# Attention's reciprocals: spread by a DMA of ScalarE's queue in place of a VectorE shuffle, and sent ahead of the next row of maxima

## The chip, the cores and the metric

The kernel runs on one core of a Trainium2 chip. The metric is the device time of one execution in microseconds (us), the median of three runs. A profile comes from one more execution, and its trace gives each instruction's start and duration on TensorE (PE, with its weight loads PEld), VectorE (DVE), ScalarE (ACT), GpSimd (POOL) and SyncE, whose work here is to issue DMAs (SP).

## The reference

A transformer layer of float32 on x of shape (2, 512, 512): attention with 32 heads of 16 columns behind a layer norm, then a mixture of 8 experts (two per token, 800 hidden columns) behind another.

```python
q, k, v = (proj(w_q), proj(w_k), proj(w_v))
scores = jnp.einsum('bhqd,bhkd->bhqk', q, k) / jnp.sqrt(jnp.float32(D_K))
attn = jax.nn.softmax(scores, axis=-1)
out = jnp.einsum('bhqk,bhkd->bhqd', attn, v)
...
x = x + _L0_attn_ref(_layernorm(x, axis=-1), L0_attn_w_q, L0_attn_w_k, L0_attn_w_v, L0_attn_w_o)
x = x + _L0_ffn_ref(_layernorm(x, axis=-1), L0_ffn_gate_w, L0_ffn_w1, L0_ffn_w2, L0_ffn_w3)
```

## The kernel before, in words

The first 97 us compute q, k and v, the last 280 us the experts. Between them lies the attention stage, in 16 head groups (`NG`) of four heads of one batch entry. Every engine has its own program, written out by hand, and engines wait for each other by semaphores that count. For one head group g:

- TensorE multiplies keys and queries once for the row maxima: 16 blocks of 128 x 512 (`key_max`, L762), into one of three banks of PSUM. VectorE reduces each block to 128 negated maxima (`maximum`, L1450). A transpose (`max_t`, L753), a copy by ScalarE (`maxima`, L1184, to max_rows) and two DMAs of SyncE (L487) lay them as one more row of the stacked queries.
- TensorE multiplies again, with keys in the rows and the maximum taken off by that row (`scores`, L774): 8 pairs of matmuls, into two pairs of banks in turn. ScalarE takes the exponential of each pair (L1234, 128 x 1024), 8 to a group. A pair of banks is free again for the scores two further when its exponential is done.
- TensorE multiplies the exponentials with the values (`pv`, L743): four P·V blocks, into ps_o. v_ones holds a column of ones beside each column of v, so the odd rows of ps_o carry the sums of the softmax.
- ScalarE copies ps_o to o_raw (L1219). SyncE brings the sums of four heads from o_raw to sum_rec, 128 x 16 (L501). VectorE takes the reciprocal (L1510). SyncE lays the reciprocals out as four rows of rec_row, 1 x 512 each, in partitions 1, 33, 65 and 97 (L495). VectorE's `stream_shuffle` (L1525) copies each of them to the 32 partitions around it, into rec_all.
- GpSimd multiplies o_raw by rec_all (L645, o_norm), SyncE brings the even partitions of o_norm into o_all, kept in q_hi's memory (L522), and GpSimd splits pairs of groups for the projection behind the stage (L659, L661).

All of this runs as a pipeline over steps s. In step s TensorE and ScalarE work on scores and exponentials of group s, VectorE on the maxima of group s + 2, and the reciprocals are those of group s - 2. TensorE's order is the list `steps` of pairs (a, b): a counts quarters of the maxima, b quarters of the scores, and in each pair TensorE issues two `key_max`, one P·V block, one `key_max`, two score matmuls, one `key_max` and two score matmuls. Up to pair 28 (`AHEAD`) both counts are equal. There a quarter without maxima is put in, and from then on the scores run one quarter ahead of the maxima. In steps 2 to 7 (groups 0 to 5) the reciprocal therefore falls one quarter before the third exponential of its step; in steps 8 to 13 (groups 6 to 11) it falls into the same quarter.

ScalarE's order in a step: exponentials 1 and 2, o_raw of the group before, (in the first half the copy of the maxima's row,) exponential 3, 4, (in the second half that copy,) exponentials 5 to 8.

SyncE's order in a step: the maxima's row of group s + 1, the reciprocals' row of group s - 2, the sums of group s - 1, up to 12 transfers of the next stacks of q and k (128 KB each), the transfer of o_norm of group s - 2, and in steps 14 and 15 a load of half of x1 from HBM (1 MB, L531), which VectorE's `residual` (L1491) waits for. SyncE waits in this order too: for the maxima's row before it looks at the reciprocals.

## Time and profile before

| | |
|---|---|
| median of three runs | 565.57 us (565.06 to 565.7) |
| the profiled execution | 566.67 us, span 564.9 us |
| TensorE busy | 539.6 us (96%) |
| VectorE busy | 393.6 us (70%) |
| ScalarE busy | 324.4 us (57%) |
| GpSimd busy | 126.0 us (22%) |
| attention stage | about 97 to 283 us |

The span is the time from the first to the last instruction in the trace; the execution's own time has 1.8 us more around it. Busy shares are averages over the whole program. Matmuls are pipelined and their ends are modelled, so TensorE's busy time holds short waits as well; the idle time of its weight loads (PEld) shows what it waited for. Start and duration of a DMA instruction are those of its issue by the engine's queue; when the data have landed is seen in the chain of waits, as "DMA".

### The profile page before, as it was taken

To read this page: it belongs to the slowest core of one execution; us is meant where nothing else is said; L and a number is where in the kernel's file an instruction comes from. 1 tells how busy PE (TensorE), PEld (TensorE's weight loads), DVE (VectorE), ACT (ScalarE), POOL (GpSimd) and SP (SyncE) were. 2 spreads that over 40 slices of the span, in tenths; PEclk is the share of its full clock that TensorE was granted. 3 is DMA by queue.
4 is the path that set the end of the run, shared out by engine and by line. 5 is a ranking of instruction groups with operands and counts; after the bars stand their busy time and mean duration, and the time that the engine had idled before them with its cause. 6 is when DMAs were issued, how large, how long until landed. Compare 5 with 4: busy or idle time off the path is not lost.

```text
span 564.9 us, 9754 instructions
## 1 busy us (share of the span) xinstructions
PE 539.6 (96%) x3504; PEld 391.7 (69%) x3504; DVE 393.6 (70%) x730; ACT 324.4 (57%) x480; POOL 126.0 (22%) x153
## 2 busy tenths in 40 slices
PE   7999999999999999999998999999999999999991
PEld 6887665333333333333667988999999999999981
DVE  6915656999998999971689887664828465666650
ACT  4322114778778777777246463747657565757540
POOL 3300111000230202452201203234341321331202
PEclk9999998999999999999999999999999999999997
DMA  8290367927456762002384499594664758586122
GB/s 317 112 112 1 56 90 80 114 42 92 71 87 80 88 82 89 20 14 87 109 303 130 175 337 351 147 329 77 248 189 140 268 148 282 99 291 170 43 32 36
DMA packets 31117, 78.19 MB, mean 138 GB/s; under 512 B 9693, under 2 KB 10973, under 8 KB 26587
## 3 DMA queue, kind: packets, MB, share of 16 engines
q1 hardware_dynamic: 25770, 68.84, 46.4%
q0 software_dynamic: 5296, 8.69, 8.4%
q8 instruction: 30, 0.49, 0.4%
q14 instruction: 21, 0.16, 0.1%
HBM read 53.11 MB, written 9.32 MB: 111 GB/s over the span
## 4 chain that ended last, share of the span: by engine, by line
PE 73%; DVE 12%; DMA 6%; issue 3%; POOL 2%; ACT 1%; SPq 1%; POOLq 0%; ACTq 0%; DVEq 0%
PE ps L731 15%; PE ps L733 14%; PE ps L732 14%; DVE neg_max L1450 7%; PE ps_o L743 7%; PE ps L762 6%; PE ps_m L762 3%; PE ps L774 3%; DMA rec_row<-sum_rec 2%; PE ps L799 2%; DMA x<-x 1%; DMA w_sb<-w 1%; DVE rec_all L1525 1%; POOL o_norm L645 1%; PE ps_o L731 1%
## 5 line engine op out<-in xcount | busy, mean ns | idle before, releaser
L1234 ACT ACTIVATE probs_t<-ps 128x1024 f32<-128x1024 f32 x128 | 124.1, 1022 | 36.1 <-PE ps L774 35.5
L1450 DVE TENSOR_REDUCE neg_max<-ps 128x1 f32<-128x512 f32 x170 | 111.7, 684 | 12.3 <-PE ps L762 10.2
L731 PE MATMUL ps<-xgT_hi,w_hi 128*128 128x256 f32 (+7 forms) x384 | 110.9, 289 | 0.9 <-DVE xgT_lo L1712 0.8
L733 PE MATMUL ps<-xgT_hi,w_lo 128*128 128x256 f32 (+7 forms) x384 | 109.7, 286 | 0.0
L732 PE MATMUL ps<-xgT_lo,w_hi 128*128 128x256 f32 (+7 forms) x384 | 109.7, 286 | 0.0
L762 PE MATMUL ps<-k_stack,q_stack 48*128 48x512 f32 x170 | 71.5, 459 | 3.6 <-issue 1.1
L731 PEld LDWEIGHTS ps<-xgT_hi,w_hi 128*128 128x128 f32 x384 | 72.7, 189 | 1.7 <-DVE xgT_lo L1712 1.3
L732 PEld LDWEIGHTS ps<-xgT_lo,w_hi 128*128 128x128 f32 x384 | 72.8, 189 | 0.1
L733 PEld LDWEIGHTS ps<-xgT_hi,w_lo 128*128 128x128 f32 x384 | 72.7, 189 | 0.0
L743 PE MATMUL ps_o<-probs_t,v_ones 128*32 128x512 f32 x512 | 68.2, 605 | 0.0
L1729 DVE TENSOR_TENSOR act<-gate,ps 128x256 f32<-128x256 f32 (+7 forms) x48 | 20.7, 431 | 67.2 <-PE ps L733 51.4
L762 PEld LDWEIGHTS ps<-k_stack,q_stack 48*128 48x128 f32 x170 | 28.8, 185 | 52.9 <-DVE neg_max L1450 41.8
L774 PE MATMUL ps<-q_stack,k_stack 49*128 49x512 f32 x256 | 63.3, 431 | 0.4 <-ACT probs_t L1234 0.4
L1450 DVE TENSOR_REDUCE neg_max<-ps_m 128x1 f32<-128x512 f32 x86 | 58.9, 684 | 4.5 <-PE ps_m L762 4.1
L1555 DVE TENSOR_TENSOR w_lo<-w_sb,w_hi 128x1024 fp32r<-128x1024 f32 x48 | 56.5, 1218 | 0.0
L1308 ACT ACTIVATE gate<-ps 128x256 f32<-128x256 f32 (+7 forms) x48 | 18.8, 392 | 61.2 <-PE ps L733 60.4
L1256 ACT ACTIVATE w_hi<-w_sb 128x1024 fp32r<-128x1024 f32 x48 | 48.6, 1056 | 3.7 <-DMA w_sb<-w 3.6
L645 POOL TENSOR_TENSOR o_norm<-o_raw,rec_all 128x512 f32<-128x512 f32 x15 | 19.2, 1283 | 101.8 <-DVE rec_all L1525 101.8
L762 PE MATMUL ps_m<-k_stack,q_stack 48*128 48x512 f32 x86 | 39.9, 464 | 1.1 <-DMA q_stack<-max_rows 0.4
L774 PEld LDWEIGHTS ps<-q_stack,k_stack 49*128 49x128 f32 x256 | 30.9, 187 | 12.0 <-ACT probs_t L1234 8.6
L691 POOL DMA_INDIRECT out<-xn,to_now x20 | 33.8, 1691 | 6.5 <-issue 6.5
L762 PEld LDWEIGHTS ps_m<-k_stack,q_stack 48*128 48x128 f32 x86 | 15.9, 185 | 27.1 <-DVE neg_max L1450 22.9
(323 smaller groups left out, 984.9 us busy)
## 6 DMA issues: line engine op xcount, KB each, us to landing
w_sb<-w SPq DMA_DIRECT2D x16, 1024.0 KB
w_sb<-w SPq DMA_DIRECT2D x8, 1536.0 KB
w_sb<-w SPq DMA_DIRECT2D x8, 1152.0 KB
q_stack<-q_hi SPq DMA_DIRECT2D x32, 128.0 KB, 5.3
k_stack<-k_hi SPq DMA_DIRECT2D x32, 128.0 KB, 5.0
q_stack<-q_lo SPq DMA_DIRECT2D x16, 128.0 KB, 4.5
k_stack<-k_lo SPq DMA_DIRECT2D x16, 128.0 KB, 6.1
q_hi<-o_norm SPq DMA_DIRECT2D x16, 128.0 KB, 3.9
```

The source lines that it names most:

```text
L645: pool.tensor_tensor(o_norm[:, g % 2, :], o_raw[:, g % 2, :], rec_all[:, :], ALU.mult).then_inc(s_on, 1)
L691: pool.indirect_dma_start(out=out[:, :], out_offset=bass.IndirectOffsetOnAxis(ap=to_now[0:rows, m:m + 1], axis=0), in_=y_sb[0:rows, m, :], ...
L731: pe.matmul(o, x_hi, w_hi, start=start, stop=False)
L732: pe.matmul(o, x_hi, w_lo, start=False, stop=False)
L733: return pe.matmul(o, x_lo, w_hi, start=False, stop=stop)
L743: last = pe.matmul(ps_o[32 * j:32 * j + 32, :], v_ones[:, (g // 8) * TPB + kc, (g % 8) * GH + j, :, :].rearrange("p d o -> p (d o)"), prob ...
L762: pe.matmul(max_bank(g, u2), q[:, qt * P:(qt + 1) * P], k, start=True, stop=True).then_inc(s_sn, 1)
L774: last = pe.matmul(ps4[:, 2 * (n % 2) + c, :], k[:, kc * P:(kc + 1) * P], q, start=True, stop=True)
L1234: a.activation(probs_t[:, kc % 2, 2 * half:2 * half + 2, :], ps4[:, 2 * (n % 2):2 * (n % 2) + 2, :], ACT.Exp, scale=D ** -0.5).then_inc(s_ ...
L1256: a.activation(w13_hi[:, at], w13_sb[:, at], ACT.Copy).then_inc(s_hi13, 1)
L1450: v.tensor_reduce(neg_max[:, g % 2, col:col + 1], max_bank(g, u2), AX.X, ALU.max, negate=True).then_inc(s_mx, 1)
L1555: v.tensor_tensor(w13_lo[:, at], w13_sb[:, at], w13_hi[:, at].bitcast(f32), ALU.subtract).then_inc(s_lo13, 1)
```

## The change

ScalarE's program gets a DMA in each of steps 2 to 15, behind the third exponential: it waits for the reciprocals' row of group s - 2 and for the o_norm before, and copies each of the four rows 16 times, to the even partitions of rec_all (64 rows of 2 KB). GpSimd waits for that transfer in place of the shuffle. For the groups 14 and 15 the shuffle stays. GpSimd fills rec_all with ones once before, so that the odd partitions hold something. And SyncE's step begins with the reciprocals' row, ahead of the maxima's row. The semaphore s_wide counts the new transfers.

```diff
+SPREAD = NG - 2
+SPREAD_AT = 2
...
             for s in range(-4, NG + 2):
+                g = s - 2
+                if 0 <= g < NG:
+                    sp.wait_ge(s_rc, g + 1)
+                    if g >= 1:
+                        sp.wait_ge(s_wide, 16 * min(g, SPREAD))
+                    if g > SPREAD:
+                        sp.wait_ge(s_sh, g - SPREAD)
+                    sp.dma_start(rec_row[1:P:2 * D, :], sum_rec[:, g % 2, :]).then_inc(s_rb, 16)
                 g = s + 1
                 if 0 <= g < NG:
                     sp.wait_ge(s_mr, g + 1)
...
-                g = s - 2
-                if 0 <= g < NG:
-                    sp.wait_ge(s_rc, g + 1)
-                    if g >= 1:
-                        sp.wait_ge(s_sh, g)
-                    sp.dma_start(rec_row[1:P:2 * D, :], sum_rec[:, g % 2, :]).then_inc(s_rb, 16)
...
             prepare(3)
+            pool.memset(rec_all[:, :], 1.0).then_inc(s_ones, 1)
 
             for g in range(NG - 1):
-                pool.wait_ge(s_sh, g + 1)
+                if g < SPREAD:
+                    pool.wait_ge(s_wide, 16 * (g + 1))
+                else:
+                    pool.wait_ge(s_sh, g - SPREAD + 1)
...
                         a.activation(probs_t[:, kc % 2, 2 * half:2 * half + 2, :], ps4[:, 2 * (n % 2):2 * (n % 2) + 2, :],
                                      ACT.Exp, scale=D ** -0.5).then_inc(s_ex, 1)
+                    if u == SPREAD_AT and 0 <= s - 2 < SPREAD:
+                        g = s - 2
+                        a.wait_ge(s_rb, 16 * (g + 1))
+                        if g == 0:
+                            a.wait_ge(s_ones, RING + 1)
+                        else:
+                            a.wait_ge(s_on, g)
+                        a.dma_start(rec_all[0:P:2, :],
+                                    rec_row[1:P:2 * D, :].unsqueeze(1).broadcast_to([GH, D, S])).then_inc(s_wide, 16)
...
-                    if u2 == 11 and g >= 0:
+                    if u2 == 11 and g >= SPREAD:
                         v.wait_ge(s_rb, 16 * (g + 1))
-                        if g >= 1:
-                            v.wait_ge(s_on, g)
+                        v.wait_ge(s_on, g)
                         v.stream_shuffle(rec_all[:, :], rec_row[:, :], [1] * 32).then_inc(s_sh, 1)
 
-            v.wait_ge(s_sh, NG)
+            v.wait_ge(s_sh, NG - SPREAD)
```

On SyncE, around the border of two steps in the second half, the order before was (the line numbers are those of each kernel; a size stands behind the names of target and source):

```order
L522 DMA q_hi<-o_norm 64x512
L487 DMA q_stack<-max_rows 1x8x128 x2
L495 DMA rec_row<-sum_rec 4x32x16
L501 DMA sum_rec<-o_raw 128x1x16
L522 DMA q_hi<-o_norm 64x512
L525 DMA q_lo<-wo 128x2048
```

In the changed kernel it is:

```order
L527 DMA q_hi<-o_norm 64x512
L492 DMA rec_row<-sum_rec 4x32x16
L498 DMA q_stack<-max_rows 1x8x128 x2
L506 DMA sum_rec<-o_raw 128x1x16
L527 DMA q_hi<-o_norm 64x512
L530 DMA q_lo<-wo 128x2048
```

The reciprocals' row has moved up past the two DMAs of the maxima's row, and stands directly behind the transfer that ends a step.

On ScalarE, in a step of the second half, the order before was:

```order
L1219 ACTIVATE o_raw<-ps_o 128x512
L1234 ACTIVATE probs_t<-ps 128x1024 x2
L1184 ACTIVATE max_rows<-ps 16x128
L1234 ACTIVATE probs_t<-ps 128x1024 x6
L1219 ACTIVATE o_raw<-ps_o 128x512
```

In the changed kernel it is:

```order
L1228 ACTIVATE o_raw<-ps_o 128x512
L1243 ACTIVATE probs_t<-ps 128x1024
L1252 DMA rec_all<-rec_row 64x1x512
L1243 ACTIVATE probs_t<-ps 128x1024
L1193 ACTIVATE max_rows<-ps 16x128
L1243 ACTIVATE probs_t<-ps 128x1024 x6
```

The DMA stands between the third and the fourth exponential, and everything of ScalarE behind it waits when it waits.

## Rows read from the trace of the kernel before

**Rows 1.** The page: busy time, the chain that ended last, DMA issues

```profile
PE 539.6 (96%) x3504; PEld 391.7 (69%) x3504; DVE 393.6 (70%) x730; ACT 324.4 (57%) x480; POOL 126.0 (22%) x153
...
PE 73%; DVE 12%; DMA 6%; issue 3%; POOL 2%; ACT 1%; SPq 1%; POOLq 0%; ACTq 0%; DVEq 0%
PE ps L731 15%; PE ps L733 14%; PE ps L732 14%; DVE neg_max L1450 7%; PE ps_o L743 7%; PE ps L762 6%; PE ps_m L762 3%; PE ps L774 3%; DMA rec_row<-sum_rec 2%; PE ps L799 2%; DMA x<-x 1%; DMA w_sb<-w 1%; DVE rec_all L1525 1%; POOL o_norm L645 1%; PE ps_o L731 1%
...
k_stack<-k_lo SPq DMA_DIRECT2D x16, 128.0 KB, 6.1
```

**Rows 2.** Stretches: length, busy of each engine, clock, DMA share, GB/s

```profile
130.83:133.53 2.70, 2.62 (x19) 0.95 (x17) 2.70 (x5) 2.27 (x3) 0.00 (x0) 1.00 0.06 9
133.53:136.57 3.04, 3.00 (x18) 1.11 (x17) 3.04 (x7) 2.28 (x4) 1.28 (x1) 1.00 0.71 125
214.08:217.10 3.02, 2.92 (x18) 1.11 (x17) 3.02 (x7) 2.27 (x4) 1.46 (x2) 1.00 0.04 5
```

**Rows 3.** Groups of VectorE's instructions, 122 to 240 us

```profile
L1525 DVE STREAM_SHUFFLE rec_all<-rec_row 128x512 f32<-128x512 f32 x11 | 8.2, 747 | 0.0
```

**Rows 4.** TensorE in order of time: start, duration, line, count

```profile
210.81 0.40 PE L774 MATMUL ps<-q_stack,k_stack 49*128 49x512 f32 x1
...
212.37 0.73 PE L774 MATMUL ps<-q_stack,k_stack 49*128 49x512 f32 x2
```

**Rows 5.** ScalarE in order of time, first and second half

```profile
130.30 1.94 ACT L1234 ACTIVATE probs_t<-ps 128x1024 f32<-128x1024 f32 x2 [0.23 <-PE ps L774]
...
207.73 1.94 ACT L1234 ACTIVATE probs_t<-ps 128x1024 f32<-128x1024 f32 x2
210.34 0.27 ACT L1184 ACTIVATE max_rows<-ps 16x128 fp32r<-16x128 f32 x1 [0.67 <-PE ps L753]
...
213.21 1.94 ACT L1234 ACTIVATE probs_t<-ps 128x1024 f32<-128x1024 f32 x2 [0.44 <-PE ps L774]
```

**Rows 6.** VectorE in order of time

```profile
207.12 0.25 DVE L1510 RECIPROCAL sum_rec<-sum_rec 128x16 f32<-128x16 f32 x1
...
250.93 0.23 DVE L1510 RECIPROCAL sum_rec<-sum_rec 128x16 f32<-128x16 f32 x1
```

**Rows 7.** SyncE's DMA issues in order of time

```profile
130.09 1.45 SPq L487 DMA_DIRECT2D q_stack<-max_rows  x2
...
206.21 0.60 SPq L522 DMA_DIRECT2D q_hi<-o_norm  x1
210.63 1.44 SPq L487 DMA_DIRECT2D q_stack<-max_rows  x2
212.18 0.59 SPq L495 DMA_DIRECT2D rec_row<-sum_rec  x1
```

**Rows 8.** TensorE's weight loads in order of time, with idle and releaser

```profile
213.26 0.18 PEld L762 LDWEIGHTS ps<-k_stack,q_stack 48*128 48x128 f32 x1 [0.25 <-DMA q_stack<-max_rows]
```

**Rows 9.** The chain that ended last: start, duration, what

```profile
189.87 1.83 DMA rec_row<-sum_rec
...
256.23 1.29 POOL o_norm L645
...
258.10 7.14 DMA x<-x
...
266.81 1.29 POOL o_norm L645
...
269.35 4.89 DMA rec_row<-sum_rec
```

**Rows 10.** DMA, 249 to 253 us: packets and share; size and us to landing

```profile
DMA packets 80, 0.13 MB, mean 33 GB/s; under 512 B 16, under 2 KB 16, under 8 KB 80
...
q1 hardware_dynamic: 80, 0.13, 8.7%
...
q_hi<-o_norm SPq DMA_DIRECT2D x1, 128.0 KB, 2.6
```

**Rows 11.** ScalarE in order of time, 262.7 us

```profile
262.80 1.02 ACT L1234 ACTIVATE probs_t<-ps 128x1024 f32<-128x1024 f32 x1
```

More of the change, by code:

```diff
@@ L260, in moe_layer @@
         s_sh = sem("s_sh")
+        s_wide = sem("s_wide")
         s_on = sem("s_on")
```

## The prediction

> **What bounds the kernel now.** I read the page first [rows 1]: TensorE is busy for 96% of the span, VectorE for 70%, and the chain that ended last is 73% TensorE and 12% VectorE, with the row maxima (L1450) as VectorE's largest line. So TensorE is the bound, but VectorE stands in the chain. The change lies in the attention stage, so the next view was the table of stretches, cut at the starts of successive P·V blocks (L743), of which a head group has four [rows 2]. An ordinary stretch takes 2.70 us, the one with the shuffle 3.03, and VectorE is busy in all of it. The reader is to see that TensorE sets 2.70 us and that the 0.747 us shuffle [rows 3] adds only 0.33 us to a head group, since VectorE catches up in the other three stretches.
>
> Third, the order of time in one head group of the second half of the stage [rows 4 to 8]. ScalarE, SyncE and TensorE hang closely together there: ScalarE copies the maxima's row at 210.34, SyncE sends it at 210.63, and TensorE's first key block of the next group waits for it at 213.26, with 0.25 us of idle weight load. That wait has no slack. It is the most important thing in the profile for this change.
>
> Last, the chain from 255 us on [rows 9]: after the maxima end, the stage's end is set not by TensorE but by o_norm, the load of x1 and the reciprocals' rows, one after another.
>
> **The sum, part by part.** Times are of the profiled execution (span 564.9, own time 566.67); the differences are applied to the median of 565.57.
>
> *Shuffles taken away.* 14 of 16 go. 11 of them lie in 122 to 240 us [rows 3], where maxima run beside them: 11 x (3.03 - 2.70) = 3.6 us. The twelfth meets the last maxima and the other two none, with TensorE at work: nothing. Bounds: 3.6, and 0 if the 3.03 were TensorE's own need; but VectorE's 3.04 of 3.04 us speaks for the shuffle.
>
> *The reciprocals' row sent first.* SyncE ends the last transfer of its step (L522) at 206.81 and the reciprocal ends at 207.12 + 0.25 = 207.37 [rows 6, 7]. The old kernel then waits for the maxima's row and sends the reciprocals at 212.18. The new one sends them at 207.40, and a lone row lands 1.83 us later [rows 9], at 209.23. The maxima's row finds SyncE free again at 208.0, long before 210.63. The edit costs nothing by itself, since SyncE was idle.
>
> *The issue on ScalarE, first half (six groups).* The reciprocal comes a whole stretch before ScalarE's third exponential (L1234), so the wait is met when ScalarE reaches it. The exponential before the issue runs for 0.92 us (1.94 - 1.02, rows 5), and an issue of 0.59 fits behind it. I take 0. Below it nothing is to be had, as ScalarE loses no work; the most is 0.31 a group, worked out under the rivals.
>
> *The issue on ScalarE, second half (six groups).* Here ScalarE's steps run one stretch ahead of the maxima, so the third exponential falls into the stretch of the reciprocal itself. It starts at 207.73 and the fourth at 208.65 [rows 5]. ScalarE now waits behind the third until 209.23, and issues. No DMA is issued by ScalarE in this trace; nearest are SyncE's, 0.57 to 0.60 us each, 0.72 for one of the maxima's pair [rows 7]. Bounds 0 and 0.72; I take 0.59, that of the row that is sent to rec_row. The fourth exponential starts at 209.26 + 0.59 + 0.10 = 209.95 in place of 208.65, and ends 1.02 later, at 210.97. Two things wait for it. The second pair of score matmuls needs its bank; a pair takes 0.73 [rows 4], so it ends at 210.97 + 0.06 + 0.73 = 211.76, where it ended at 210.81 + 0.40 = 211.21: 0.55 late. And the copy of the maxima's row, next on ScalarE, starts at 209.95 + 0.92 = 210.87 in place of 210.34, 0.53 late, and TensorE already waits for that row [rows 8]. Both delays are the same time on TensorE, not two: 0.55. ScalarE makes it good before the next group, as it idles 0.44 us before the pair at 213.21. 6 x 0.55 = 3.3 us; with an issue of 0 us it is 0, with 0.72 it is 4.1.
>
> *The transfer and o_norm.* GpSimd now waits for 128 KB. The nearest row, a lone transfer of 128 KB, lands after 2.6 us [rows 10]. Of its 80 packets 64 are of 2 KB; 8.7% of 16 engines in 4 us is 0.087 us for each of these. The new source lies in 4 partitions. If it is spread over 4 engines in place of 16, each carries 16 packets and not 4: 12 x 0.087 = 1.0 more, 3.6 us. The upper bound is the 6.1 us of k_stack<-k_lo, last of six in a queue [rows 1]. I take 3.6: the queue of ScalarE is empty, so it is near the lone row, and its source is narrow. In the steady groups it is hidden: issued at 209.26 it lands at 212.9, before the stretch of the shuffle at 214.08.
>
> The Trainium skill (DMA: Bandwidth & Descriptors, section on why a DMA increments its semaphore by 16 and not by 1) says that the number of engines is the largest up to 16 that divides the slowest dimension of both sides; here these are 4 and 64, so 4. By that rule the 3.6 us stand, without it 2.6; no row here shows the engines of one transfer.
>
> *The tail.* The reciprocals of 250.93 end at 251.16 [rows 6], are sent at 251.19 and land at 253.02; ScalarE issues at 253.05, and at 256.65 they are spread. The o_norm of that group, at 256.23 before [rows 9], starts at 256.69. The load of x1 behind it moves from 258.10 to 258.56, and the next row goes 0.67 later, at 259.23. Behind such a load a row takes 4.89 [rows 9]: landed at 264.12. ScalarE waits for exactly this row in its next step, behind the third exponential of 262.80 [rows 11]; it issues at 264.15 and the spread lands at 267.75, where o_norm had started at 266.81: +1.0 us. From there the chain is serial to the end of the stage. TensorE is held too, as the fourth exponential starts at 264.84 and not at 263.72, but this is the same microsecond. Bounds of the term: with a landing of 2.6 us o_norm is at 255.7, the row lands at 263.1 and the next spread at 265.8, -1.0; with 6.1 us twice, +6.
>
> Sum: -3.6 + 0 + 3.3 + 1.0 = +0.7 us: 566.3 (profiled, 567.4). About 0.2%, 1.13 us, is the least that can be told from no change here.
>
> **The rivals.**
> *ScalarE's issue costs it almost nothing*: the exponentials go on beside it. Then the fourth starts at 209.4, the score pair and the maxima's row are on time, and the 3.3 become 0: -3.6 + 1.0 = -2.6, 563.0. For it: nothing in the trace shows what a compute engine pays. Against: SyncE pays near 0.6 for every size.
> *Sixteen engines*: the tail gives 1.0 back, -3.6 + 3.3 - 1.0 = -1.3, 564.3. Against it is only the narrow source.
> *The two queues get in each other's way, slower.* In the first half ScalarE's issue, at 130.30, falls into SyncE's two of the maxima's row, 130.09 to 131.54 [rows 5, 7]. If one can issue at a time, ScalarE's runs from 130.83 to 131.42, and the fourth exponential starts at 131.53, not 131.22: 0.31 us on TensorE, whose score pair waits for it, in the five groups where the rows meet: 1.5 us. It decides as soon as ScalarE's issue ends later than its third exponential. 566.3 + 1.5 = 567.8. For it: the issues stand close; against: no row has two queues issuing at once.
> The Trainium skill (Perfetto Trace Analysis, DMA Instruction — HWDGE) says that the block that makes descriptors is shared and locked for one engine at a time. That is this rival; by the rule the sum is 567.8, without it 566.3.
> *The shuffle's 0.33 does not come back*, because TensorE's own need fills it: 3.6 more, 569.9. VectorE's full stretch speaks against it.
> That the row isn't sent ahead at all, because SyncE still waits for o_norm of the step before, I exclude: that transfer ended at 206.81, and o_norm comes no later now.
>
> **How the numbers follow.** Forecast 0.38, its own range 565.3 to 567.4; cheap issue 0.22; sixteen engines 0.12; queues 0.18; no gain from the shuffle 0.06; anything else 0.04. Faster (under 564.44): the cheap issue, half of the sixteen engines, half of the rest and a tenth of the forecast, 0.32. Slower (over 566.70): queues, no gain, half of the rest and a quarter of the forecast, 0.36. Same: 0.32. The range runs from the cheap issue to the queues, 562.8 to 567.9; past it lie no gain from the shuffle, long landings and a part of the cheap issue, together 0.2.
>
> **What would show it.** Right: no stretch of 3.03 us; a DMA issue of ScalarE of about 0.6 us near 209, 0.6 to 1.3 us of idle ScalarE before the fourth exponential, and TensorE waiting 0.5 us for ScalarE or the maxima's row in each of six groups; o_norm 1 us later near 267 against the P·V blocks. Wrong: exponentials unmoved beside the issue (cheap issue), an issue of ScalarE or SyncE of over 1 us near 130 (queues), o_norm earlier near 267 (sixteen engines), or stretches still at 3.03. The term of which I am least sure is ScalarE's 0.59 us.

## The result, and the profile after

The changed kernel takes 588.27 us (median; 583.96 to 592.58), the kernel before 565.57: a ratio of 1.0396, 95% interval 1.0367 to 1.0425. It is slower by 22.7 us, where I had forecast + 0.7 and a range that ended at 567.9. The profiled execution is the fastest of the five: 583.96 us, span 582.2, mean granted clock 0.973. The slower ones have lower clocks (592.58 us at 0.951), so the loss has a part that varies with the clock.

The page, as in [rows 1]: busy time, the chain that ended last, its lines.

```profile
PE 543.9 (93%) x3504; PEld 393.0 (68%) x3504; DVE 387.0 (66%) x702; ACT 323.8 (56%) x480; POOL 126.6 (22%) x154
...
PE 67%; DMA 11%; DVE 7%; SPq 5%; issue 3%; POOL 2%; ACT 2%; ACTq 1%; POOLq 0%; DVEq 0%
PE ps L740 15%; PE ps L742 15%; PE ps L741 15%; DMA rec_row<-sum_rec 7%; PE ps_o L752 5%; DVE neg_max L1468 4%; PE ps L771 4%; SPq L481 3%; PE ps_m L771 2%; DMA q_stack<-max_rows 2%; PE ps L808 2%; DMA rec_all<-rec_row 1%; PE ps L783 1%; SPq L498 1%; POOL o_norm L654 1%
```

The busy times hardly differ. The chain does: the reciprocals' row has risen from 2% to 7%, SyncE's issues are on it with 5%, and VectorE has gone from 12% to 7%. The stretches between P·V blocks, with the columns of [rows 2]:

```profile
121.02:123.73 2.71, 2.63 (x18) 1.02 (x17) 2.49 (x5) 1.95 (x3) 1.27 (x1) 1.00 0.61 131
129.19:133.43 4.24, 2.41 (x19) 0.76 (x17) 2.81 (x5) 2.24 (x3) 0.00 (x0) 1.00 0.41 76
...
176.79:181.94 5.15, 3.03 (x20) 1.06 (x18) 2.67 (x4) 2.45 (x4) 0.00 (x0) 1.00 0.32 34
181.94:185.44 3.50, 3.50 (x19) 1.56 (x17) 2.76 (x5) 2.20 (x4) 1.28 (x1) 0.60 0.24 61
...
204.77:210.99 6.22, 3.48 (x19) 1.19 (x18) 2.69 (x5) 2.33 (x5) 0.00 (x0) 0.92 0.44 48
210.99:214.79 3.80, 3.71 (x19) 1.26 (x17) 2.46 (x4) 1.66 (x2) 1.27 (x1) 0.69 0.34 85
232.93:235.99 3.06, 3.04 (x19) 1.06 (x18) 2.66 (x5) 1.91 (x4) 0.00 (x0) 1.00 0.16 25
```

The first row is the place of a shuffle: 2.71 us where it was 3.03, as forecast. But the stretch with ScalarE's DMA is 4.24, 5.15 or 6.22 us, where 2.7 was forecast for the first half and 2.7 plus 0.55 for the second. Behind the two worst of them the next stretch is long too, with TensorE busy nearly throughout at a granted clock of 0.60 or 0.69. Only from 230 us on (last row) is it the small cost that I had expected.

Around the worst of them, SyncE's issues, ScalarE and TensorE in order of time, as in [rows 4, 5, 7]:

```profile
201.69 0.59 SPq L481 DMA_DIRECT2D k_stack<-k_lo  x1
202.33 0.60 SPq L527 DMA_DIRECT2D q_hi<-o_norm  x1
203.56 0.57 SPq L492 DMA_DIRECT2D rec_row<-sum_rec  x1
210.00 1.46 SPq L498 DMA_DIRECT2D q_stack<-max_rows  x2
```

```profile
203.89 1.03 ACT L1243 ACTIVATE probs_t<-ps 128x1024 f32<-128x1024 f32 x1
208.21 0.55 ACTq L1252 DMA_DIRECT2D rec_all<-rec_row  x1
208.81 1.02 ACT L1243 ACTIVATE probs_t<-ps 128x1024 f32<-128x1024 f32 x1 [3.89 <-DMA rec_row<-sum_rec]
```

```profile
209.88 0.74 PE L783 MATMUL ps<-q_stack,k_stack 49*128 49x512 f32 x2 [2.74 <-ACT probs_t L1243]
```

Here the row is sent as soon as it is made, as the change says, but ScalarE can issue only at 208.21: the row was on its way for 4.6 us and not 1.83. Its neighbours on SyncE show what has changed: the last of six stack transfers of 128 KB is issued 1.9 us before it, and o_norm's 1.2 us. The kernel before sent it 6 us behind the transfer that ends the step [rows 7]. The chain gives its durations over the stage, as in [rows 9]:

```profile
126.80 4.28 DMA rec_row<-sum_rec
149.94 5.29 DMA rec_row<-sum_rec
...
203.56 4.63 DMA rec_row<-sum_rec
...
242.90 1.81 DMA rec_row<-sum_rec
```

At 242.90 there are no more stacks to send, and it is 1.81 us again.

### The profile page after: what moved, and what is told of

It reads as the page before. It is cut to its first block, busy times and chain, and to the rows that moved or that the text cites. A ratio compares the mean times of both kernels' runs of the same rounds, so it can differ in the third digit from the quotient of the medians.

```text
span 582.2 us, 9742 instructions
## 1 busy us (share of the span) xinstructions
PE 543.9 (93%) x3504; PEld 393.0 (68%) x3504; DVE 387.0 (66%) x702; ACT 323.8 (56%) x480; POOL 126.6 (22%) x154
## 3 DMA queue, kind: packets, MB, share of 16 engines
q10 hardware_dynamic: 952, 1.84, 1.6%
## 4 chain that ended last, share of the span: by engine, by line
PE 67%; DMA 11%; DVE 7%; SPq 5%; issue 3%; POOL 2%; ACT 2%; ACTq 1%; POOLq 0%; DVEq 0%
PE ps L740 15%; PE ps L742 15%; PE ps L741 15%; DMA rec_row<-sum_rec 7%; PE ps_o L752 5%; DVE neg_max L1468 4%; PE ps L771 4%; SPq L481 3%; PE ps_m L771 2%; DMA q_stack<-max_rows 2%; PE ps L808 2%; DMA rec_all<-rec_row 1%; PE ps L783 1%; SPq L498 1%; POOL o_norm L654 1%
## 5 line engine op out<-in xcount | busy, mean ns | idle before, releaser
L783 PE MATMUL ps<-q_stack,k_stack 49*128 49x512 f32 x256 | 65.3, 457 | 12.1 <-ACT probs_t L1243 12.1
L771 PE MATMUL ps<-k_stack,q_stack 48*128 48x512 f32 x170 | 69.6, 464 | 5.0 <-DMA q_stack<-max_rows 1.7
L752 PE MATMUL ps_o<-probs_t,v_ones 128*32 128x512 f32 x512 | 71.7, 633 | 0.0
```

What stands on the lines that cost most here:

```text
L752: last = pe.matmul(ps_o[32 * j:32 * j + 32, :], v_ones[:, (g // 8) * TPB + kc, (g % 8) * GH + j, :, :].rearrange("p d o -> p (d o)"), prob ...
L771: pe.matmul(max_bank(g, u2), q[:, qt * P:(qt + 1) * P], k, start=True, stop=True).then_inc(s_sn, 1)
L783: last = pe.matmul(ps4[:, 2 * (n % 2) + c, :], k[:, kc * P:(kc + 1) * P], q, start=True, stop=True)
```

## The experiments

Times are medians of runs beside runs of the kernel before. In four kernels (1, 6, 10, 15) other values reach the experts, whose share of the work then changes, so only the attention stage compares there. "The stage" is the time from the start of the first P·V block to the start of the last in the profiled run, by the table of stretches. It is one execution of each kernel, and the changed kernel's five executions lie 8.6 us apart as a whole, so a difference of stages is rough where TensorE stalls. Landings of the row and of the narrow transfer (ScalarE's, out of 4 partitions) are those of the last semaphore event that the trace records for them.

| kernel | stage us | its clock | ratio to before (95%) |
|---|---|---|---|
| before | 172.8 | 1.00 | |
| after | 188.3 | 0.95 | 1.0396 (1.0367 to 1.0425) |
| 3 row first | 172.4 | 1.00 | 0.999 (0.9969 to 1.001) |
| 6 no shuffle | 169.2 | 1.00 | |
| 9 row by ScalarE's queue | 173.1 | 1.00 | 1.0012 (0.9985 to 1.0038) |
| 5 wait alone | 181.2 | 0.96 | 1.0153 (1.0126 to 1.018) |
| 1 small stacks | 172.4 | 1.00 | |
| 10 small spread | 182.4 | 0.95 | |
| 15 wide source | 181.3 | 0.96 | |
| 13 first half alone | 185.5 | 0.94 | 1.0172 (1.014 to 1.0205) |
| 11, 12, 4: spread at 3, 4, 5 | 191.2, 196.0, 195.2 | 0.90 | 1.0314, 1.045, 1.0581 |
| 7 SyncE spreads | 184.9 | 0.95 | 1.0238 (1.0202 to 1.0273) |
| 8 SyncE spreads, other order | 187.8 | 0.94 | 1.043 (1.0385 to 1.0475) |
| 14 stacks behind the row | 199.1 | 0.89 | 1.0439 (1.04 to 1.0478) |
| 2 row by GpSimd | 217.2 | 0.86 | 1.0867 (1.0835 to 1.09) |
| 16 four rows, 6 groups | 171.5 | 1.00 | 1.001 (0.9992 to 1.0027) |
| 17 four rows, 5 groups | 170.8 | 1.00 | 0.9948 (0.9928 to 0.9967) |
| 18 four rows, 12 groups | 171.1 | 1.00 | 0.9952 (0.9932 to 0.9971) |

### Is the row late because of the stacks?

**1, small stacks.**

```diff
+                w = T // B if pair < RING else 64
...
-                            sp.dma_start(to[at][dst, :, :].bitcast(f32),
+                            sp.dma_start(to[at][dst, :, 0:w].bitcast(f32),
```

> The changed kernel, but from pair 4 of the stacked queries and keys on only 64 of the 512 columns are copied (16 KB in place of 128 KB for each of the transfers behind the sums; the scores of groups 8 to 15 are then computed from partly old stacks). Theory A (behind the stacks: the reciprocals' row is sent directly behind six 128 KB transfers of SyncE's queue and lands 3.6 to 5.3 us after its issue, ScalarE waits for it in order, TensorE for ScalarE, and the clock falls after the stalls): the row lands 1.8 to 2.3 us after its issue in every group, the P.V stretch with ScalarE's DMA is at most 3.1 us as in groups 11 to 13 of the changed kernel, the granted clock is 1.00 throughout the stage; 565.6 - 3.6 + 6 x 0.25 + 1.0 = 564.5, range 562.5 to 567. Theory B (two issuing queues in each other's way, whatever the sizes): the stretches of 3.6 to 6.2 us stay, 580 or more. Theory C (ScalarE's issue or its own transfer is the cost): the time stays over 575.

The row lands after 1.80 to 2.14 us in groups 0 to 12. From step 2 to step 7 there is no long stretch at all, the clock is 1.00, and steps 8 to 13 show the price of ScalarE's issue itself, 2.94 to 3.02 us where a stretch of this place takes 2.75:

```profile
205.22:208.20 2.98, 2.98 (x18) 1.05 (x18) 2.58 (x5) 1.90 (x4) 1.88 (x2) 1.00 0.14 29
```

Theory A is right, C is out as the main cause. But C is not nothing. Two more stretches are long, 3.39 us at 185.29 and 3.23 at 208.20, because TensorE waits there for the maxima's row, as shown under 10 and 15. The stage takes 172.4 us against 172.8 before, so even with a prompt row the change gains next to nothing. The time of the whole (608.58) says nothing.

**3, row first.** The new order of SyncE in the kernel before, shuffle kept.

> The kernel before with SyncE's new order alone: the reciprocals' row ahead of the maxima's row, the spreading still by VectorE's shuffle at its old place. Theory A: the row lands late here too, 3.6 to 5 us after its issue where stacks are in the queue, but nobody waits for it in order until the shuffle, over 6 us later; TensorE and the clock are as before and the time is 565.6, range 564.5 to 566.5. A rival, by which the row's place disturbs the maxima's row (which TensorE waits for without slack): the maxima's row lands later, up to 0.5 us in each of six groups, 568.5.

563.56 against 564.13 us: the same. The rows of groups 1 to 9 land after 3.85 to 4.54 us, those of groups 10 to 12, behind no stacks, after 1.81 to 1.83. When the late ones are sent, three to five large transfers have not yet landed. So the order alone makes the row late and costs nothing while nobody waits for it.

**5, wait alone.**

```diff
+                    if u == 2 and 0 <= s - 2 < NG - 2:
+                        a.wait_ge(s_rb, 16 * (s - 1))
```

> The kernel before with the reciprocals' row sent first, as in experiment 3, and one wait more: behind the third exponential ScalarE waits for that row, and does nothing with it. No DMA on ScalarE, no spreading transfer, VectorE's shuffles all there. Theory A (the late row, waited for in ScalarE's order, is what costs): the first P.V stretches of the groups are 3.6 to 6 us where stacks are on their way, as in the changed kernel, the granted clock falls behind the worst of them, and the time is 563.6 + 15 to 25 = 578 to 590. Theory C (the issue and the 128 KB transfer cost, the wait alone is nothing): 565.

573.83 us, + 9.1, where 578 to 590 was expected; the stage is 8.8 us longer than with the row first. Step 8:

```profile
184.39:188.94 4.55, 3.02 (x19) 1.06 (x18) 2.70 (x5) 1.91 (x4) 1.60 (x2) 1.00 0.38 35
188.94:192.23 3.29, 3.29 (x19) 1.58 (x17) 2.75 (x6) 2.20 (x4) 0.29 (x1) 0.65 0.11 29
192.23:196.39 4.16, 4.16 (x18) 1.65 (x17) 3.05 (x6) 1.94 (x4) 1.27 (x1) 0.50 1.00 133
196.39:200.40 4.01, 4.01 (x18) 1.65 (x17) 2.65 (x6) 2.38 (x4) 0.00 (x0) 0.53 0.73 75
```

TensorE waits for an exponential and the stretch is 1.8 us longer than in 3. Then three stretches run at a granted clock of 0.65, 0.50 and 0.53; 0.50 is 1.2 GHz, the lower of its two levels, and this stretch takes 4.16 us there in place of 3.02 in 3. The three stalls of this run come to 5.0 us and the slow stretches behind them to 3.9. But all three lie in the second half: in the first, where ScalarE comes to the wait later, there is none, and the changed kernel has four (4.24, 3.61, 4.21 and 5.15 us). Half of its loss was thus not explained.

**2 and 9, the row by another queue.** In 2 GpSimd sends the row of groups 0 to 13 in the changed kernel; in 9 ScalarE sends that of groups 0 to 5 in experiment 3, from an empty queue.

```diff
+                    if u == 0 and 0 <= s - 2 < NG // 2 - 2:
+                        g = s - 2
+                        a.wait_ge(s_rc, g + 1)
...
+                        a.dma_start(rec_row[1:P:2 * D, :], sum_rec[:, g % 2, :]).then_inc(s_rb, 16)
```

> The changed kernel, with the reciprocals' row of groups 0 to 13 sent by GpSimd's queue, as soon as the reciprocal is there; SyncE sends the last two. ScalarE's DMA stays behind the third exponential, the six stack transfers stay in SyncE's queue. Theory A1 (the row is late because it stands behind the stacks in the same queue): it lands 1.9 to 2.8 us after its issue with the stacks still on their way, ScalarE's wait behind the third exponential shrinks from up to 3.9 us to at most 1 us in the second half and to nothing in the first, and the time is 565 to 570. Theory A2 (the row is late because the 16 DMA engines are busy with the stacks, from whatever queue it comes): it lands 3.6 to 5 us after its issue as before, and the time stays at 580 or more. Theory B (two queues): three queues now issue, 588 or more.

> Experiment 3 (row first, shuffle kept), but in steps 2 to 7 the reciprocals' row is issued by ScalarE, ahead of its first exponential, at the moment at which SyncE issued it there (125.30 us for group 1); ScalarE's queue is empty. Theory A1 (late because of its own queue, behind the stacks in order): the rows of groups 1 to 5 land after 1.8 to 1.9 us. Theory A2 (late because the DMA engines serve the stacks of all queues): they land after 3.5 to 4.5 us as in experiment 3. The time is that of experiment 3 within 1.5 us either way, as the shuffle comes 6 us later.

In 9 (565.44, ratio 1.0012, interval 0.9985 to 1.0038) the rows of groups 1 to 5 land 4.70, 4.16, 4.13, 4.00 and 3.81 us after their issue, in 3 it is 4.36, 4.14, 4.12, 3.93 and 3.85. The queue makes no difference: I had taken the row to stand behind the stacks in SyncE's own queue, and that is refuted. The packets of the row sent at 125.97 show where its time goes. The first line is the DMA of 9 from 125.97 to 128.90 us, the second its ScalarE queue (q10) from 128.90 to 129.70; columns are packets, MB, share of 16 engines:

```profile
q1 hardware_dynamic: 196, 0.33, 106.2%
...
q10 hardware_dynamic: 132, 0.01, 30.6%
```

For 3.0 us after its issue the empty queue moves nothing, while SyncE's transfers fill the engines. All its packets fall between 128.97 and 129.67, and the row has landed at 130.67. A lone row of 3 (sent at 227.83) has its first packet after 1.2 us and lands 0.3 us behind its last. So most of the delay lies ahead of the row's own data, and about 0.7 us behind them. The Trainium skill (DMA: Bandwidth & Descriptors, Queues, rings and completion order) says that the semaphore write of a DMA lands only after every earlier write of the same DMA engine, across its queues. The trace agrees in that the row is late from an empty queue too (4.70 us), but this rule bears on the last 0.7 us alone; why the packets start late was not looked into further. Experiment 2 (613.05 us, where 565 to 570 was expected) shows the same for GpSimd's queue: 5.4 us for the row sent at 174.62 beside stacks issued from 172.45 to 176.28, 2.2 us for the one sent at 188.61 without. It also sends late, behind GpSimd's other work, so its time tells nothing more.

### What does the spreading transfer do?

**10 and 15, fewer bytes; as many from a wide source.** The first spreads 64 of 512 columns. The second moves 128 KB to the same 64 partitions, but out of 64 and not out of 4.

```diff
-                                    rec_row[1:P:2 * D, :].unsqueeze(1).broadcast_to([GH, D, S])).then_inc(s_wide, 16)
+                                    rec_row[1:P:2, :]).then_inc(s_wide, 16)
```

> The changed kernel, but ScalarE's transfer spreads only 64 of the 512 columns (16 KB in place of 128; o_norm is divided in an eighth of its columns only). Its issue, ScalarE's wait for the row and the order are as in the changed kernel. The stage (first P.V block to the end of the last) took 172.4 us with the row first and shuffles, 188.3 in the changed kernel, 181.2 with the wait alone. Theory D (the rest of the cost comes from the transfer's length: it makes o_norm late, SyncE waits for o_norm before it sends the next row, and so the next row is late as well): the stage takes about 181.2 - 3.3 + 6 x 0.25 = 179.4 us, rows are sent every 11 us and land after 4.1 us. The rival (the length does not matter, the issue on ScalarE does): 186 to 189.

> The changed kernel, but ScalarE's transfer of 128 KB reads 64 partitions of rec_row, one for each row of rec_all, in place of 4 partitions 16 times (the size and the target are the same, most of what it spreads is no reciprocal, so o_norm is not divided rightly). What is open is whether the transfer's 4.2 to 6.2 us, and SyncE's stack issues of 2.0 us beside it, come from its bytes or from its narrow source. By the narrow source: it lands after 2.6 to 3.5 us, SyncE's issues are 0.6 us, the first half is nearly clean, and the stage takes 182 to 184 us as with an eighth of the columns. By its bytes: 186 to 189 us and long issues as in the changed kernel.

The stage takes 182.4 and 181.3 us, near the 181.2 of the wait alone and 6 to 7 less than in the changed kernel. In the changed kernel the transfer takes 4.2 us alone and up to 6.2 beside stacks; here it is 1.83 to 2.12 in 10, and in 15

```profile
rec_all<-rec_row ACTq DMA_DIRECT2D x7, 128.0 KB, 2.0
```

(the last number is the median from issue to landing). The trace has 5 semaphore events for each narrow transfer, the first of them within 1 us of the start of its issue, and 16 for each wide one. That the other four are those of four engines is the rule that the prediction drew on, and the landings bear it out. What I had not foreseen is what it does to other DMAs. First to SyncE's issues, in the changed kernel and then in 15, behind ScalarE's issue at 131.10 and 132.40:

```profile
130.62 0.64 SPq L481 DMA_DIRECT2D q_stack<-q_hi  x1
131.30 0.59 SPq L481 DMA_DIRECT2D k_stack<-k_hi  x1
131.93 2.05 SPq L481 DMA_DIRECT2D q_stack<-q_lo  x1
134.03 2.04 SPq L481 DMA_DIRECT2D k_stack<-k_hi  x1
136.11 0.59 SPq L481 DMA_DIRECT2D q_stack<-q_hi  x1
```

```profile
133.77 0.59 SPq L481 DMA_DIRECT2D k_stack<-k_hi  x1
134.41 0.59 SPq L481 DMA_DIRECT2D q_stack<-q_lo  x1
135.04 0.60 SPq L481 DMA_DIRECT2D k_stack<-k_hi  x1
135.69 0.60 SPq L481 DMA_DIRECT2D q_stack<-q_hi  x1
```

While the narrow transfer is on its way two of SyncE's issues take 2.05 us and not 0.6. In the whole stage 9 of 48 issues that fall into such a flight take over 1.3 us, and none of 21 and 25 in 10 and 15. But the narrow transfer is not the only cause: one of 1.92 us stands at 124.13, where the first transfer had landed at 122.30, and experiment 6, which spreads nothing, has the same one:

```profile
123.77 1.86 SPq L478 DMA_DIRECT2D k_stack<-k_lo  x1
```

Second, the landing itself makes o_norm late, and SyncE sends o_norm before the next row. The transfer of 131.10 lands at 137.27, and the next row, whose reciprocal ends at 137.60, goes at 139.26:

```profile
137.33 1.28 POOL L654 TENSOR_TENSOR o_norm<-o_raw,rec_all 128x512 f32<-128x512 f32 x1 [13.68 <-DMA rec_all<-rec_row]
...
138.64 0.52 SPq L527 DMA_DIRECT2D q_hi<-o_norm  x1
139.26 0.58 SPq L492 DMA_DIRECT2D rec_row<-sum_rec  x1
```

In the changed kernel the rows of groups 2 and 4 wait like this for o_norm and those of groups 1, 3 and 5 for SyncE's issues, 0.5 to 1.7 us behind their reciprocals; in 3, 10 and 15 each of them goes at once. That brings the row to ScalarE's wait in the first half too.

Third, the maxima's row, which TensorE awaits without slack. In the second half it is sent while the narrow transfer is in flight and lands 2.0 to 2.6 us after its second issue, where it is 1.8 in 10 and 15. TensorE waits 2.7 us for it in the stage, against 0.4 in the kernel before and 0.5 in 10 and in 15.

The issue at 131.30 overlaps ScalarE's at 131.10 and neither is longer, and so it is at 142.89, 155.25 and 265.91. The rival of the prediction said that the two queues lock each other out in issuing, as the Trainium skill has it (Perfetto Trace Analysis, DMA Instruction — HWDGE); no such lengthening is seen here.

**13, first half alone.** `SPREAD = NG // 2 - 2`.

> The changed kernel with ScalarE's spreading for groups 0 to 5 alone; from group 6 on the shuffle, as before. By the theory as it stands (stacks in flight make the row land after 4 us; ScalarE is not held in the first half by that alone; the spreading transfer, 4.2 us alone and 5 to 6 beside the next stacks, makes o_norm and then the next row late): the first half loses what it loses in the changed kernel, 1.5 + 0.9 + 1.5 us and some clock, less 5 x 0.33 for the shuffles; the second half is that of the kernel before. 564.6 + 4 to 5 - 1.6 = 567.5, range 566 to 570. If the loss were in the second half alone: 563.

574.31 us, ratio 1.0172; expected 567.5. The mechanism is there (rows sent late, landing after 3.6 to 4.2 us, stretches of 4.39, 4.20, 3.54 and 5.30), the size is not: I had left most of the clock out once more. Behind the last stall stand four stretches of 4.16 to 4.90 us at a granted clock of 0.50.

### Where in the order could it stand?

**7 and 8, SyncE spreads.** In both ScalarE's DMA is gone and groups 12 to 15 keep the shuffle. In 7 the order is row, maxima's row, spread, sums, stacks, o_norm; in 8 maxima's row, row, o_norm of the group before, sums, spread, stacks.

```diff
+                if 0 <= s - 2 < SPREAD:
+                    g = s - 2
+                    sp.wait_ge(s_rb, 16 * (g + 1))
...
+                    sp.dma_start(rec_all[0:P:2, :],
+                                rec_row[1:P:2 * D, :].unsqueeze(1).broadcast_to([GH, D, S])).then_inc(s_wide, 16)
```

> The changed kernel with the spreading transfer of groups 0 to 11 issued by SyncE, behind the maxima's row and ahead of the sums; ScalarE issues and waits for nothing; groups 12 to 15 keep the shuffle. The reciprocals' row is still sent first and still lands 4 us after its issue. Theory A: only SyncE waits for it, where it idles anyway, so TensorE sees nothing: 564.1 - 3.6 + 0 to 1 = 561.0, range 559.5 to 564. The rival (the transfer, 4.2 us alone and 6 beside stacks, makes o_norm so late that SyncE reaches the next maxima's row late): 0.5 to 2 us in each of 12 groups, 570 or more.

> The kernel before with the spreading by a SyncE transfer for groups 0 to 11, ordered so that nothing waits where it hurts: the maxima's row, the reciprocals' row (alone on its way as in the kernel before, 1.83 us), the o_norm transfer of the group before, the sums, then the spreading transfer, then the stacks. No shuffle beside the maxima, no DMA on ScalarE. Theory A: every wait of SyncE is met, stretches of 2.70 to 2.76 throughout, the granted clock 1.00: 564.1 - 3.6 = 560.5, range 559.5 to 562.5. The rival, that a 128 KB transfer from four partitions beside the stacks is late whoever issues it and holds SyncE or o_raw up: 566 or more.

577.87 us (ratio 1.0238) and 588.24 us (1.043), both far off the 561.0 and 560.5 expected. The rivals won, each with its own wait. In 7 the sums now stand behind a wait and reach VectorE late; in 8, where most rows land after 1.84 us, o_norm is late for o_raw of the next group but one, which shares its buffer:

```profile
DVE sum_rec L1528 <- DMA sum_rec<-o_raw: 6.3, 6, 2.3
```

```profile
ACT o_raw L1242 <- POOL o_norm L668: 15.9, 9, 3.1
PE ps_o L766 <- ACT o_raw L1242: 7.6, 6, 2.1
```

(Waits: who, for whom; us in all, times, longest.) The spread takes 4.3 us in 7 and 4.2 to 5.4 in 8; the row lands after up to 5.6 us in 7.

**4, 11, 12, the place on ScalarE.** `SPREAD_AT` = 5, 3 and 4.

> The changed kernel with ScalarE's DMA behind the sixth exponential of its step in place of the third (one number). Theory A: the sixth exponential ends 3.9 us or more after the third, so the row, which lands 3.6 to 5.3 us after its issue, is there or nearly; ScalarE waits 0 to 0.5 us, no P.V stretch is over 3.2 us, the granted clock is 1.00; o_norm comes 3 us later in the tail. 565.6 - 3.6 + 0 to 1.5 for the issues + 2.5 for the tail = 565.0, range 562.5 to 567.5. Theory B or C (queues or the issue and transfer themselves): the cost doesn't depend on the place, 580 or more.

> The changed kernel with ScalarE's DMA behind the fourth exponential in place of the third. Theory A with two bounds: too early, ScalarE waits for the late row; too late, o_raw of the next group waits for o_norm. Here in the first half no wait, as the fourth exponential ends 0.9 us later than the third; in the second half the wait is 1 us shorter. Between the changed kernel (third, 584 to 588) and nothing lost: 570 to 580, I say 576.

> The changed kernel with ScalarE's DMA behind the fifth exponential. Theory A with two bounds: in the second half the fifth ends at about 211.8 on the clock of the kernel before, when the row (sent 207.4, 4.1 us) has landed, so no wait; issued at 211.8 the transfer lands at 216.5 to 217.5, o_norm ends at 218.3, and o_raw, which waits for it, is due at 218.2: just met. In the first half o_norm ends 1 us or more too late for o_raw. 568 to 580, I say 573; behind the sixth it was 598 (in time with the kernel before at 564.1). If ScalarE's place did not matter, 585.

597.96, 583.72 (1.0263 to 1.0365) and 593.65 us. My numbers were 565, 576 and 573: wrong by 33, 8 and 21 us, in the direction that a second bound exists. ScalarE's wait for the row shrinks (3.4 us in 4, 14.7 in the changed kernel), but the o_norm deadline is missed:

```profile
ACT o_raw L1228 <- POOL o_norm L654: 10.8, 8, 3.3
```

With a narrow transfer none of the four places tried lies between the two bounds. For 12 I had taken 4.7 to 5.7 us; beside stacks it was 4.5 to 6.9.

**14, stacks behind the row.** As 13, with the stacks ahead of the maxima's row in steps 2 to 7.

```diff
+                if 2 <= s < NG // 2:
+                    if s % 2 == 0:
+                        ready((s + 6) // 2)
+                    stack((s + 6) // 2, [s % 2], "qk")
                 g = s + 1
```

> As experiment 13, with one change of order on SyncE in steps 2 to 7: the six stack transfers stand directly behind the reciprocals' row, ahead of the maxima's row, in a gap in which SyncE idled. So no stack is in flight when the next row is sent, and the spreading transfer overlaps only their end. The maxima's row goes 1.3 us later, but has 5.7 us to spare in this half. Theory: rows 1 to 5 land after 1.8 to 2.3 us, the spread after 4.2 to 5, no stall in the first half, no shuffle in it: 564.6 - 5 x 0.33 = 563.0, range 562 to 564.3. Rival (the spreading transfer or ScalarE's issue costs by itself in this half): 566 or more.

589.29 us, where 563.0 was expected. The row does land after 1.81 to 1.89 us, but the maxima's row has taken its place behind the stacks, and TensorE waits for that one up to 5.1 us:

```profile
PE ps L775 <- DMA q_stack<-max_rows: 13.5, 4, 5.1
```

My 5.7 us of slack were wrong. Taking a small transfer out of the stacks' way by putting another into it is no gain.

### The ceiling, and versions that are faster

**6, no shuffle.**

```diff
-                    if u2 == 11 and g >= 0:
+                    if u2 == 11 and g >= NG - 2:
```

> The kernel before without the 14 shuffles of groups 0 to 13 and with nothing in their place: o_norm of these groups is multiplied by ones, so they are not divided by their sums; the reciprocals' rows are still sent. It gives the most that the change could bring. My sum said 11 x 0.33 = 3.6 us: 560.5 against 564.1. The rival, by which the 3.03 us stretches are TensorE's own need, says 564.1.

The stage takes 169.2 us, 3.6 less than in the kernel before and 3.3 less than in 3: all that the change could bring.

**16, 17 and 18, four rows.** SyncE writes the row of reciprocals four times, so that the spread reads 16 partitions. 16 does so for groups 0 to 5 behind the fourth exponential, 17 for groups 0 to 4, 18 for groups 0 to 11, behind the fifth from step 7 on.

```diff
+                    for c in range(4 if g < SPREAD else 1):
+                        sp.dma_start(rec_row[1 + 8 * c:P:2 * D, :], sum_rec[:, g % 2, :]).then_inc(s_rb, 16)
...
-                                    rec_row[1:P:2 * D, :].unsqueeze(1).broadcast_to([GH, D, S])).then_inc(s_wide, 16)
+                                    rec_row[1:P:8, :].unsqueeze(1).broadcast_to([4 * GH, D // 4, S])).then_inc(s_wide, 16)
```

> A version that takes the causes away in the half in which ScalarE has slack: ScalarE's spreading for groups 0 to 5 alone, behind the fourth exponential, from 16 partitions: SyncE writes the reciprocals' row four times (to partitions 1, 9, 17 and 25 of each head), in the 3 us in which it idles ahead of the maxima's row. From group 6 on the row goes once and the shuffle stands. If the narrow source is the cause of the long transfer and of SyncE's long issues: the last row is sent at +1.9 us and lands 4 us later, at the end of the fourth exponential, the spread takes 2.6 to 3.5 us, nothing is late, 564.3 - 5 x 0.33 = 562.7, range 561.5 to 564.5. If not, or if the four rows hold the maxima's row up: 568 or more, near the 574.3 of experiment 13.

> As experiment 16, for groups 0 to 4 alone. In 16 one stretch of 3.83 us stood in step 7, where the maxima's copy on ScalarE waited behind the DMA for the row (that step has the quarter in which the order of scores and maxima shifts); the rest of the half was at 2.70. Without group 5 that stretch is gone and one shuffle comes back: 171.5 - 1.07 + 0.3 = 170.8 us for the stage against 172.4, and 564.2 - 1.5 = 562.7, range 561.5 to 564.

> As experiment 16, for groups 0 to 11: behind the fourth exponential in steps 2 to 6 and behind the fifth from step 7 on, where the fourth copy of the row, sent 1.8 us after the first, has landed (209.0 against a first one sent at 204.65). All 11 shuffles beside maxima are gone, - 3.6. The issue pushes the sixth exponential back by 0.55, at 0.25 us on TensorE in each of six groups, + 1.5; stage 170.3, time 562.1, range 560.5 to 565. Rival: the four row issues leave SyncE no room ahead of the maxima's row, which TensorE waits for without slack: 0.5 or more in each of six groups, 566 or more.

16 takes 565.26 us, where 562.7 was expected: its stage takes 171.5, its first half runs at the ordinary length but for one stretch of 3.84 us in step 7, and the whole is the same as before within the measurement. 17 takes 561.85 us and 18 562.38: both are faster than the kernel before by half a per cent, with intervals that leave out 1, and not told apart. A stretch of 17 that had a shuffle, and its SyncE with four rows in the gap:

```profile
132.82:135.51 2.69, 2.62 (x17) 1.02 (x16) 2.47 (x5) 2.06 (x3) 0.84 (x1) 1.00 1.01 171
```

```profile
126.15 2.34 SPq L493 DMA_DIRECT2D rec_row<-sum_rec  x4
129.38 1.40 SPq L499 DMA_DIRECT2D q_stack<-max_rows  x2
```

In 18 the second half keeps stretches of 2.94 to 3.37 us where ScalarE issues, and in the longest of them it still waits 1.1 us for the row; that eats what it gains on the shuffles there. 11 and 12, with the narrow transfer at the same two places of ScalarE's order but in 14 groups, took 583.72 and 593.65 us.

## Why the prediction was wrong

The prediction said 566.3 us; 588.27 was measured. By its own steps:

- *Shuffles taken away*, - 3.6: right, 3.6 by experiment 6 against the kernel before, 3.3 against 3.
- *The row sent first*, "a lone row lands 1.83 us later": this is the step that failed. The row moved from 6 us behind the transfer that ends the step to 1 to 2 us behind it and was not alone. It lands after 3.85 to 4.54 us (3), late from an empty queue too (9). The row for it stood in front of me: k_stack<-k_lo, 6.1 us [rows 1], issued at 201.69 in the changed kernel, is still landing 4 us after the row is sent. I used it for the spread alone.
- *The issue, first half*, 0: right for the issue (2.70 us in experiment 1), wrong for the wait, which the late row meets there as well.
- *The issue, second half*, 6 x 0.55 = 3.3: its 0.59 us is 0.53 to 0.55 in the trace, and TensorE loses about 0.25 of it and not 0.55, 1.5 us in all. The wait in front of it is what costs: 8.8 us for the stage (5), of which 3.9 stand in stretches at a low clock.
- *The transfer*, 3.6 us and hidden: 4.2 alone, up to 6.2 beside stacks. Four engines was right, "hidden" was not. Its landing holds up o_norm and with it the next row, its flight goes with SyncE issues of up to 2.08 us and with a maxima's row that lands late. 5.9 us of the stage are gone with an eighth of its bytes (10), one execution of each.
- *"o_norm comes no later now"*, by which I excluded that the row is held up: false, o_norm holds up the rows of groups 2 and 4.
- *The tail*, + 1.0: near. The stretch at 277 us is 3.33 us in place of 2.55.
- *The chances*: those for "faster" add up to 0.34 by their own list, not 0.32; nothing hangs on it.
- *The clock* had no term. In the changed kernel six stretches behind stalls, at granted clocks of 0.50 to 0.78, are 5.7 us longer than ordinary ones. A stall of TensorE has to be costed with the stretches behind it.

In the stage: 172.4 with the row first, - 3.3, + 1.5, + 0.8 for the tail, + 8.8 and + 5.9 make 186.1; 188.3 was measured. The remaining 2 us are not assigned, and the term of 5.9 is rough; the parts aren't strictly additive, as stalls and clock depend on each other. The rest of the 17.3 us by which the spans differ lies in the chain behind the stage.

Of the rivals, the two queues in each other's way named the right pair of engines, and its sign, a SyncE issue of over 1 us near 130, came true; but for another reason, and its price of 1.5 us was far too low.

## What to carry to other kernels

A transfer's time from issue to landing belongs to the moment at which it is sent: when a small, urgent one is moved, look at what large ones were issued in the 4 us before its new place (here on another queue too), and take its landing from a row with the same company. Before an engine that feeds TensorE is given an in-order wait, it must have slack for the late case, and a stall can be paid twice, once as such and once in the clock. A transfer that nobody waits for can still delay one that somebody does. A broadcast by DMA is better read from many partitions: three more small issues in an idle gap made the spread short enough for the idea to pay, by half a per cent.

## What the runs showed of the hardware

- A row of 8 KB lands 1.8 us after its issue alone and 3.8 to 4.7 us with four or five transfers of 128 KB not yet landed, whether SyncE or ScalarE issues it (3, 9). From ScalarE's empty queue its first packet goes 2.1 to 3.0 us after the issue, 1.2 alone (3).
- 128 KB to 64 partitions: 4.2 us out of 4 partitions, 2.0 out of 64, 2.2 to 3.4 in all but one case out of 16 (16).
- While the transfer out of 4 partitions is in flight, some of SyncE's issues take 1.4 to 2.7 us in place of 0.6 (9 of 48 in the changed kernel, up to 2.65 in 11), behind a spread of its own queue too (7: 2.0 us for the second issue behind it). Single ones stand without such a transfer as well (6: 1.86 us). The cause was not looked into further.
- The second DMA of the maxima's row lands after 1.8 us, and after 2.0 to 2.6 beside the transfer out of 4 partitions (changed kernel, second half).
- A DMA issue on ScalarE takes 0.53 to 0.55 us between two exponentials in the changed kernel, 0.47 in 15; the first one of the changed kernel takes 1.24.
